# One ScalarE softplus for a chain of eight steps, one more product on VectorE, and engine programs without loops

## The reference

```python
xh = silu(causal_conv_k2(xh, conv_w, conv_b))          # 256 channels
x_dbl = xh @ W_x                                       # 8 + 16 + 16 columns
dt = softplus(dt_low @ W_dt + b_dt)                    # 256 channels
A = -exp(A_log)                                        # 256 x 16 states
def step(h, inp):
    dA = exp(dt_t[..., None] * A)
    dBx = dt_t[..., None] * B_t[:, None, :] * x_t[..., None]
    h = dA * h + dBx
    y = einsum('bdn,bn->bd', h, C_t)
y = (y + xc * D) * silu(z);   out = y @ W_out
```

## Time and profile before

| | |
|---|---|
| median of three executions | 18219.49 us |
| the profiled execution | 18229.67 us, its span 18227.6 us |
| VectorE busy | 14628.5 us (80%) |
| GpSimd busy | 13648.5 us (75%) |
| TensorE busy | 15233.1 us (84%), mean granted clock 0.898 of full |
| ScalarE busy | 10286.6 us (56%) |

### The profile page before, as it was taken

One profiled execution on the slowest core, in us unless ns is written; L12 is line 12 of the kernel. 1 busy time (PEld: TensorE's weight loads), 2 busy tenths in 40 slices (PEclk: granted clock), 3 DMA queues, 4 the chain that ended last, 5 costly groups with the idle time before them and its releaser, 6 DMA issues. The chain is left out here.

```text
span 18227.6 us, 188137 instructions
## 1 busy us (share of the span) xinstructions
PE 15233.1 (84%) x40250; PEld 5585.0 (31%) x40250; DVE 14628.5 (80%) x14056; ACT 10286.6 (56%) x14202; POOL 13648.5 (75%) x5902
## 2 busy tenths in 40 slices
PE   8999999777788888888888888888888888888876
PEld 2333333222233333333333333333333333233322
DVE  1111111599999999999999999999999999999952
ACT  1222222466666666666666666666666666666642
POOL 0000000399999999999999999999999999999940
PEclk9999999899998888888888888888888888888865
DMA  1101110244444444444444444444444444444445
GB/s 38 33 27 32 29 28 21 85 161 162 159 155 164 162 157 161 163 159 162 156 162 157 164 160 158 163 158 159 159 164 159 157 164 162 155 157 164 162 180 210
DMA packets 508191, 2499.22 MB, mean 137 GB/s; under 512 B 53097, under 2 KB 164938, under 8 KB 226651
## 3 DMA queue, kind: packets, MB, share of 16 engines
q1 hardware_dynamic: 489723, 2419.71, 35.8%
q10 hardware_dynamic: 18208, 76.11, 1.1%
HBM read 2325.05 MB, written 170.57 MB: 137 GB/s over the span
## 5 line engine op out<-in xcount | busy, mean ns | idle before, releaser
L718 POOL TENSOR_TENSOR hc<-h,c_all 128x1024 f32<-128x1024 f32 x4096 | 9526.9, 2355 | 278.5 <-PE y_ps L959 271.3
L959 PE MATMUL y_ps<-hc,ident 128*128 128x512 f32 x16392 | 8002.9, 632 | 932.1 <-POOL hc L718 931.8
L834 ACT ACTIVATE d_a<-dt,a_neg 128x512 f32<-128x512 f32 x8194 | 5596.3, 688 | 4252.4 <-DVE h L1063 4203.0
L1063 DVE TENSOR_TENSOR_SCAN h<-d_a,h,dbx_v 128x512 f32<-128x512 f32 x4960 | 6100.8, 1268 | 24.4
L959 PEld LDWEIGHTS y_ps<-hc,ident 128*128 128x128 f32 x16392 | 3158.7, 202 | 5895.4 <-issue 3803.8
L707 POOL TENSOR_TENSOR dbx_p<-dtx,b_all 128x1024 f32<-128x1024 f32 x1536 | 3616.0, 2354 | 185.1 <-DVE h L1063 184.5
L1063 DVE TENSOR_TENSOR_SCAN h<-d_a,h,dbx_p 128x512 f32<-128x512 f32 x2976 | 3660.7, 1267 | 43.1 <-ACT d_a L834 38.5
L1050 DVE TENSOR_TENSOR dbx_v<-dtx_ps,b_all 128x1024 f32<-128x1024 f32 x2560 | 3021.6, 1207 | 13.1 <-issue 9.5
L463 POOL MEMSET ident_f<- 128x128 f32 x1 | 0.2, 205 | 3350.9 <-POOLq L44 3350.9
L346 DVE RECIPROCAL k_inv<-k_nrm 128x4 f32<-128x4 f32 x256 | 45.5, 178 | 2686.2 <-ACT k_nrm L211 2686.2
L271 PE MATMUL conv_ps<-image,w_taps 128*32 128x512 f32 x11520 | 1775.2, 594 | 0.0
(11 more groups left out here) (128 smaller groups left out, 10841.0 us busy)
## 6 DMA issues: line engine op xcount, KB each, us to landing
b_all<-bc_dram SPq DMA_DIRECT2D x1028, 1024.0 KB, 6.9
c_all<-bc_dram SPq DMA_DIRECT2D x1025, 1024.0 KB, 4.7
o_dram<-o_sb SPq DMA_DIRECT2D x257, 256.0 KB, 7.4
o_t<-o_dram SPq DMA_DIRECT2D x64, 1024.0 KB, 9.9
out<-r_t ACTq DMA_DIRECT2D x64, 1024.0 KB, 9.2
image<-in_x SPq DMA_DIRECT2D x91, 512.0 KB, 4.1
un<-un_dram SPq DMA_DIRECT2D x516, 34.0 KB
bc_dram<-low_bc SPq DMA_DIRECT2D x257, 64.0 KB, 4.5
```

Of the source, the lines that this page charges most:

```text
L718: nc.gpsimd.tensor_tensor(hc[:, n % HC], h[:, n], c_all[:, n // CG % 2, n % CG].unsqueeze(1).broadcast_to([128, 2, CH]), ALU.mult).then_in ...
L834: nc.scalar.activation(d_a[:, half], dt[:, p, half], ACT.Exp, scale=a_neg[:, half, n:n + 1]).then_inc(a_done, 1)
L959: last = nc.tensor.matmul(y_ps[:, half], ident[:], hc[:, n % HC, half], start=False, stop=(n == S - 1))
L1063: nc.vector.tensor_tensor_scan(h[:, n, half], d_a[:, half], dbx, zero_col[:] if first else h[:, n, half, CH - 1:CH], ALU.mult, ALU.add).th ...
```

## The change

Three things change. The first replaces the eight steps of softplus by one ScalarE function, which reads `p_ps`, adds the bias and writes `dt` directly. It needs its own table of function values: ScalarE loads that before and reloads the table of exp after. The second takes state 14 from GpSimd's list, so that GpSimd makes 5 drive products of 16 in a chunk and VectorE 11. The third writes every `Fori` out as a Python `range`, so counts of waits are constants. The orders in `body` change as well.

```diff
-ON_POOL = [7, 9, 11, 13, 14, 15]
+ON_POOL = [7, 9, 11, 13, 15]
...
         def chunks(eng, body):
-            with eng.Fori(0, B) as b:
+            for b in range(0, B):
                 body(b, b * NCH, b * (NCH // 2), 0, 0, True, False)
-                with eng.Fori(0, NCH // 2 - 1) as j:
+                for j in range(0, NCH // 2 - 1):
...
 GpSimd, body:
-                weigh(km, 7)
                 weigh_out(km, 0)
                 weigh_out(km, 1)
+                weigh_out(km, 2)
+                weigh(km, 7)
                 weigh(km, 9)
-                weigh_out(km, 2)
                 weigh_out(km, 3)
                 weigh_out(km, 4)
-                weigh(km, 11)
                 weigh_out(km, 5)
                 weigh_out(km, 6)
+                weigh(km, 11)
                 weigh_out(km, 7)
+                weigh_out(km, 8)
                 weigh(km, 13)
-                weigh_out(km, 8)
-                weigh(km, 14)
-                make_dtx(km, 1 - p)
-                weigh(km, 15)
                 weigh_out(km, 9)
                 weigh_out(km, 10)
                 weigh_out(km, 11)
+                weigh(km, 15)
+                make_dtx(km, 1 - p)
                 weigh_out(km, 12)
...
 ScalarE: biased, absolute, exponential, plus_one and logarithm go, and
+            def softplus(km, p):
+                after(act, "a_done", 2 * S * km)
+                after(act, "dtx_done", km)
+                for half in range(2):
+                    after(act, f"dt_mm{half}", km + 2)
+                    last = nc.scalar.activation(dt[:, p, half], p_ps[:, half], ACT.Softplus, bias=b_dt[:, half:half + 1])
+                last.then_inc(dt_done, 1)
+                nc.scalar.preload_act_table_set("natural_log_exp_and_others")
...
 ScalarE, body: silu_x moves from behind decay 4 to behind decay 2, low from behind 7 to behind 6,
 rows from between the halves of 8 to behind 8, copy_out from within 14 to behind 12,
 copy_dtx from behind 14 to behind 15; and
                 decay(km, 10, 0, p)
-                biased(km, 1)
-                absolute(km)
                 decay(km, 10, 1, p)
-                exponential(km)
+                softplus(km, q)
                 decay(km, 11, 0, p)
...
 TensorE, body:
                 add_skip(km, p)
-                project_x(km, q)
                 add_state(km, 0)
                 add_state(km, 1)
                 add_state(km, 2)
-                project_dt(km, 0)
-                project_dt(km, 1)
+                project_x(km, q)
                 add_state(km, 3)
                 add_state(km, 4)
                 add_state(km, 5)
+                project_dt(km, 0)
+                project_dt(km, 1)
...
 VectorE, body: positive, rounding and make_dt go, and
                 run_scan(km, 1, 0, first)
+                run_scan(km, 1, 1, first)
                 weigh(km, 2)
-                run_scan(km, 1, 1, first)
+                weigh(km, 3)
                 run_scan(km, 2, 0, first)
-                weigh(km, 3)
                 run_scan(km, 2, 1, first)
+                gate(km, q)
+                weigh(km, 4)
                 run_scan(km, 3, 0, first)
                 run_scan(km, 3, 1, first)
-                weigh(km, 4)
-                weigh(km, 5)
                 run_scan(km, 4, 0, first)
                 run_scan(km, 4, 1, first)
-                gate(km, q)
+                weigh(km, 5)
+                weigh(km, 6)
                 run_scan(km, 5, 0, first)
                 run_scan(km, 5, 1, first)
-                weigh(km, 6)
                 weigh(km, 8)
...
                 run_scan(km, 10, 0, first)
+                run_scan(km, 10, 1, first)
                 weigh(km, 12)
-                run_scan(km, 10, 1, first)
-                positive(km)
+                weigh(km, 14)
                 run_scan(km, 11, 0, first)
```

More of the change, by code:

```diff
@@ L162, in _ @@
                 if b + 1 < B:
-                    with sp.Fori(0, PIECES - 3) as j:
+                    for j in range(0, PIECES - 3):
                         sp.wait_ge(conv_done, b * NCH + 2 * j + 7)
@@ L228, in query @@
                 act.dma_start(uq[M:KU, bass.ds(c0, CH)], s_sb[64:65, p]).then_inc(u_stored[p], 16)
-            with act.Fori(0, B) as b:
-                with act.Fori(0, NCH // 2) as j:
+            for b in range(0, B):
+                for j in range(0, NCH // 2):
                     for p in range(2):
@@ L294, in outer @@
                 last.then_inc(mat_mm, 1)
-            with pe.Fori(0, B) as b:
+            for b in range(0, B):
                 loaded(pe, b)
@@ L396, in _ @@
                         next(between)(b - 1)
-                with dve.Fori(3, NCH // 2 - 1) as j:
+                for j in range(3, NCH // 2 - 1):
                     for i in range(2):
@@ L668, in body @@
                 sp.dma_start(o_dram[:, bass.ds(km * CH, CH)], o_sb[:]).then_inc(o_stored, 16)
-            with sp.Fori(0, B) as b:
+            for b in range(0, B):
                 at = b * (SLOTS * CH) + CH
                 body(b, b * NCH, at + 2 * CH, 0, False)
-                with sp.Fori(0, NCH // 2 - 2) as j:
+                for j in range(0, NCH // 2 - 2):
                     for i in range(2):
@@ L848, in body @@
                 decay(km, 2, 1, p)
+                silu_x(km, q)
+                nc.scalar.preload_act_table_set("natural_log_exp_and_others")
                 decay(km, 3, 0, p)
@@ L852, in body @@
                 decay(km, 4, 1, p)
-                silu_x(km, q)
                 decay(km, 5, 0, p)
@@ L910, in _ @@
             after(pe, "built", 2)
-            after(pe, "consts", 11)
+            after(pe, "consts", 10)
             after(pe, "ready", 4)
@@ L1151, in body @@
                 run_scan(km, 14, 0, first)
+                run_scan(km, 14, 1, first)
                 statistics(b, km, NCH - 1 if first else c - 1)
@@ L1217, in _ @@
                 sp.sem_inc(stored[p], 16)
-            with sp.Fori(0, B) as b:
-                with sp.Fori(0, NCB // 2) as j:
+            for b in range(0, B):
+                for j in range(0, NCB // 2):
                     for p in range(2):
@@ L1231, in _ @@
             nc.scalar.activation(g_std[:], g_m2[:], ACT.Sqrt, bias=eps[:]).then_inc(rooted, 1)
-            with act.Fori(0, B) as b:
+            for b in range(0, B):
                 act.wait_ge(ab_done, 2 * b + 2)
-                with act.Fori(0, NCB // 2) as j:
+                for j in range(0, NCB // 2):
                     for p in range(2):
@@ L1252, in _ @@
             pe.wait_ge(step, STEPS_BEFORE_ROOT)
-            with pe.Fori(0, B) as b:
-                with pe.Fori(0, NCB // 2) as j:
+            for b in range(0, B):
+                for j in range(0, NCB // 2):
                     for p in range(2):
@@ L1294, in _ @@
             dve.sem_inc(added, 2)
-            with dve.Fori(0, B) as b:
+            for b in range(0, B):
                 dve.wait_ge(silu_done, b * NCB + 2)
@@ L1302, in _ @@
                                       ).then_inc(gm_done, 1)
-                with dve.Fori(0, NCB // 2) as j:
+                for j in range(0, NCB // 2):
                     for p in range(2):
```

77 lines of the change are left out of this document (10 added, 67 removed).

## The result

The changed kernel took 17532.16 us in the median of four executions (17526.46 to 17535.72), against 18219.92 before: a ratio of 0.9622, with a 95% interval of 0.9606 to 0.9639. It is 688 us faster. None of the rivals names the cause of the difference.

The account below looks back on a forecast made before the run. VectorE was taken as the bound in phase B, GpSimd just behind; terms of -3.36 + 1.12 + 0.15 + 0.1 = -2.0 us over 256 chunks, -510 us, gave 17710 us, range 17580 to 17960.

Parts of the forecast that it names:

- What bounds the kernel: Phase B, 10 to 16 ms: VectorE is the bound with 1% idle, GpSimd right behind with 3%.
- the sum for phase B: Per chunk: -3.36 + 1.12 + 0.15 + 0.1 = -2.0 us, times 256 chunks: -510 us.
- The dependent product: VectorE's drive of state 8, directly behind the scan of 5 whose slot it overwrites, waits for its end: +0.15 us.
- The wait at the gate: VectorE's earlier gate waiting for TensorE's sum: +0.1 us a chunk in the mean, realistic upper end 1.1.
- the wait at the image ends: Gate waiting for new weights in an image's last chunk, 7.45 us before; change taken as 0, eight times.
- Softplus on ScalarE: Phase B: softplus block 4.58 us like silu_x, decays held 5.2 against 5.7 of cover; 0.4 left, cost 0.
- Rival C: Softplus holds decays beyond its cover: by 0.9 (17940, chance 0.08), about 2.0 (18220, 0.02) or 2.3 (18300, 0.02).
- The gate: VectorE, phase B: gate due at 11.6 us instead of 18.5; TensorE's half clock after idle may use up its slack.
- rival B: Gate waits on TensorE every chunk because its clock stays low: +1 us a chunk, about 17950; chance 0.17.
- The slack of 2.4: TensorE's sum ready at 61.5 us, gate due at 63.9: 2.4 us to spare at full clock.
- Loops written out: Register instructions run ahead of the engines, so removing loops gives 0 to -0.2 us a chunk; taken as 0.
- rival D: Fetching straight code stalls VectorE or GpSimd, kernel slower: +1.5 us a chunk, 18600, in its example; chance 0.07.

Follow-up runs that it names:

- one swap on GpSimd: Changed kernel with GpSimd's drive of 15 made ahead of the C product of 11 instead of behind it: 17432.21 us, 100 less than the changed kernel.

## Why the prediction was wrong

**What bounds the kernel, and the sum for phase B** were right in mechanism, and the number was met partly by luck. Net of the loops a chunk fell by 2.00 us, the number of the sum, but its terms were off both ways. Three softplus steps less and one product more are -2.24 as summed. The dependent product cost 0.2 (summed 0.15). The wait at the gate, summed at 0.1, came to 107.5 us in the 227 chunks between 4 and 16 ms (12000 us at 52.8), of which 26.5 stay at the image ends when the rest is taken away: 0.36 in an ordinary chunk. Against these went the waits at the statistics, 0.22 a chunk, which I had put only at the lower end of the range, and some of the wait at the image ends (46.0 us in 7 places with the old kernel's loops out, 26.5 in 8 now, 0.09 a chunk), which I had put at nothing. These two gains cancel the two excesses.

**Softplus on ScalarE** was right: a block of 4.59 where silu_x gave 4.58, a reserve of 0.4 behind it, and with one load of 1.28 more a delay of 0.92. By its own terms the sum leaves 5.72 - 5.23 = 0.5 where it says 0.4; the 0.4 was met all the same. (The upper bound for 1.55 a chunk is 17823, not 17830.) The Trainium skill's 1380 ns of drain at a switch ("ScalarE: Activation LUTs", What ACT_TABLE_LOAD costs) does not appear in this kernel: function follows load by 1.30 from start to start. Rival C fell.

**The gate** was right in its mechanism, the half clock behind TensorE's longest wait, and too small by a quarter of a microsecond; rival B's 1 us did not come. The slack of 2.4 was 1 us too large. The product of 12 starts on TensorE 0.5 us after VectorE's new chunk (9027.01 and 9026.49), where the sum had it 0.1 before, and the sum let the product of 13 follow at once, though by its own count that one is ready 2.3 us after 12, and TensorE needs 1.85 for 12. The clock took 1.34 of what was left.

**Loops written out** is the step that failed: "the register instructions run ahead of the engines, which stood only 1% idle, so 0 to -0.2; I take 0". It put the term at nothing for the whole program by the idle time of one phase. The 1% idle is that of VectorE in phase B. The loops are also in phase A, where TensorE is the bound, and there I had looked at one line, the largest, with 0.0 of idle before it, and not at the waits of the phase. They showed 151.9 us, 248 times, for a relu of ScalarE, and ScalarE's own list 319.3 us of "issue" ahead of that relu. What the runs show in its place: the loops were worth 125 us ahead of the first gate, 103 of them ScalarE's alone, some 30 in phase B (28.7 or 38.5, by which trace is taken for before) and 4 behind it, 159 in the medians. Without them the changed kernel stands 530 us under, where the forecast was 510. The bound of 0.2 us a chunk was exceeded in phase A, 0.5 a chunk, and held in phase B, 0.11 to 0.15.

The reason given, that register instructions run ahead of the engine, fits VectorE in phase B: with registers between its steps two products take 2.25 and a scan 1.18, and with all loops out still 2.25 (9025.30 to 9027.55) and 1.18. On ScalarE in phase A it did not hold. There the sequencer waits for the end of the square root before it issues the two DMAs (the first starts at 1119.78, the square root ends at 1118.98 + 0.59 = 1119.57), and the registers for the second DMA and for the next relu come behind that wait. That this is what keeps it from running ahead fits the rows and the code; no run tests it apart.

**Fetching straight code**, rival D: the two code queues moved 323 + 458 packets where they had moved 154 + 106, and VectorE shows no idle without a releaser in phase B (4 to 16 ms). The Trainium skill says that straight code is fetched ahead and mostly hidden ("Runtime: NRT & Kernel Launch", Instruction fetch mechanics), and this case agrees. Its other half, that a taken branch can cost a fetch, isn't shown apart from the arithmetic in any run.

## What to carry to other kernels

Price an edit in every phase that it touches, and read the waits of the engine that is the bound in each; a line with no idle says nothing about its neighbours. Registers that a sequencer computes between the steps of an engine cost little where it could run ahead, as in phase B (0.11 to 0.15 us a chunk for all loops). They cost 0.4 a chunk (103 us in 256) between two ScalarE steps on the path of TensorE, with two DMA issues between them that themselves wait for the first step. So look for places where the sequencer itself must wait, on the path of the bound. When two engines are both near full, follow the chain that leads from one over a third to the other: its order, and the longest wait in it, set how early the next step may stand.

## What the runs showed of the hardware

A ScalarE softplus of 128x512 with a bias takes 683 ns in the mean, as silu does (683), and a load of its table 1283 like any other. A VectorE instruction that must wait for the one directly ahead started 0.1 us (a product and its own scan, 1.23 from start to start for 1.12) to 0.2 us later (a scan and the product that takes its slot) than an independent one. The half clock of TensorE, through the gate, cost VectorE about 0.4 us a chunk (100 us in 256), though no VectorE instruction was slower for it (the gate's median is 1200 ns with it and 1199 without), and one swap on GpSimd took nearly all of it away.
